# Rotary position products from one projection: exchanged halves are copied by ACT instead of made by PE

## The reference, cut to what matters

```python
var = jnp.mean(jnp.square(x), axis=-1, keepdims=True)
x_norm = x * jax.lax.rsqrt(var + EPS) * norm_scale
q = (x_norm @ Wq).reshape(b, seq, n_heads, dh)
k = (x_norm @ Wk).reshape(b, seq, n_heads, dh)
v = (x_norm @ Wv).reshape(b, seq, n_heads, dh)
q = apply_rope(q); k = apply_rope(k)
...
x1, x2 = jnp.split(x, 2, axis=-1)      # in apply_rope, per head
return jnp.concatenate([x1 * cos - x2 * sin, x1 * sin + x2 * cos], axis=-1)
```

## Time and profile before

| | |
|---|---|
| median of 3 runs | 2100.53 us (2097.97 to 2101.24) |
| profiled execution, its own time | 2096.08 us |
| its span, first to last instruction | 2094.2 us |
| mean granted TensorE clock | 0.903 of full |
| PE busy | 1725.3 us (82%) |
| DVE busy | 1591.4 us (76%) |
| ACT busy | 1014.0 us (48%) |
| POOL busy | 925.0 us (44%) |

### The profile page before, as it was taken

The page is one execution under the profiler, slowest core; times in us unless marked ns, Lnnn a source line. Parts: engine busy times, 40 slices in busy tenths (PEclk is TensorE's granted clock), DMA queues, the critical chain, the costliest instruction groups (busy, mean ns, idle before and its releaser), DMA issues.

```text
span 2094.2 us, 33718 instructions
## 1 busy us (share of the span) xinstructions
PE 1725.3 (82%) x12064; PEld 1120.0 (53%) x12141; DVE 1591.4 (76%) x3386; ACT 1014.0 (48%) x1997; POOL 925.0 (44%) x1166
## 2 busy tenths in 40 slices
PE   1465889989898989889798989989798989978785
PEld 0233446565565646465565646555565646555544
DVE  2666869889797979879696979879697978874522
ACT  1143363746455463646455473745445463735151
POOL 3335253636354463636344463636445453623112
PEclk9676789999898999989898999989899999989797
DMA  3001010000101010100101010000101010000100
GB/s 91 0 5 45 7 46 6 27 27 7 51 7 47 11 46 9 38 18 7 51 7 46 12 46 6 27 31 7 51 7 46 12 46 1 22 31 8 46 12 6
DMA packets 64617, 53.34 MB, mean 25 GB/s; under 512 B 6019, under 2 KB 63171, under 8 KB 64451
## 3 DMA queue, kind: packets, MB, share of 16 engines
q1 hardware_dynamic: 64450, 51.19, 7.9%
HBM read 8.44 MB, written 4.19 MB: 6 GB/s over the span
## 4 chain that ended last, share of the span: by engine, by line
PE 45%; DVE 25%; SPq 9%; issue 7%; ACT 5%; POOL 5%; DMA 4%; DVEq 0%; ACTq 0%; POOLq 0%
PE bank L872 42%; SPq L299 8%; DVE rmax L743 7%; DMA kh<-part 4%; PE bank L868 3%; DVE prob L823 2%; DVE tree L653 2%; DVE stats L644 2%; ACT prob L464 2%; DVE rmax L740 1%; DVE inner L653 1%; SPq L311 1%; POOL rstd L343 1%; ACT xch L480 1%; DVE kk L666 1%
## 5 line engine op out<-in xcount | busy, mean ns | idle before, releaser
L743 DVE TENSOR_REDUCE rmax<-bank 128x1 f32<-128x512 f32 (+2 forms) x768 | 355.7, 504 | 131.3 <-PE bank L872 130.9
L464 ACT ACTIVATE prob<-bank 128x512 f32<-128x512 f32 x640 | 354.4, 598 | 136.1 <-PE bank L872 131.0
L872 PE MATMUL bank<-kh,qh 72*128 72x512 bf16 (+3 forms) x1024 | 289.2, 332 | 93.2 <-DMA kh<-part 52.8
L430 POOL TENSOR_TENSOR prob<-xdT,spread 128x512 f32<-128x512 f32 x128 | 167.5, 1309 | 377.4 <-ACT spread L464 377.4
L872 PE MATMUL bank<-wexpT,prob 128*128 128x128 f32 x2048 | 272.1, 279 | 5.3 <-issue 4.1
L872 PE MATMUL bank<-qh,kh 75*128 75x512 bf16 (+3 forms) x1024 | 256.6, 305 | 22.7 <-ACT prob L464 19.6
L872 PEld LDWEIGHTS bank<-wexpT,prob 128*128 128x128 f32 x2048 | 255.2, 193 | 18.5 <-issue 12.4
L872 PEld LDWEIGHTS bank<-kh,qh 72*128 72x128 bf16 x1024 | 108.5, 106 | 211.4 <-DVE rmax L743 71.8
L464 ACT ACTIVATE spread<-bank 128x512 f32<-128x512 f32 x128 | 76.5, 597 | 296.0 <-PE bank L872 209.5
L690 DVE RECIPROCAL wkb<-wkb 128x512 f32<-128x512 f32 x64 | 213.3, 3332 | 0.5 <-POOL wkb L376 0.5
L872 PE MATMUL bank<-maskb,identb 128*128 128x128 bf16 x1024 | 210.8, 237 | 0.0
(11 more groups left out here) (212 smaller groups left out, 3556.9 us busy)
## 6 DMA issues: line engine op xcount, KB each, us to landing
qh<-part SPq DMA_DIRECT2D x144, 128.0 KB
kh<-part SPq DMA_DIRECT2D x144, 128.0 KB
x<-in_L_attn_x_dram SPq DMA_DIRECT2D x16, 256.0 KB, 2.9
out_dram<-yo SPq DMA_DIRECT2D x16, 256.0 KB, 3.0
qh<-maxT SPq DMA_DIRECT2D x16, 48.0 KB
wk<-in_L_attn_tm_Wk_dram SPq DMA_DIRECT2D x1, 256.0 KB
wv<-in_L_attn_tm_Wv_dram SPq DMA_DIRECT2D x1, 256.0 KB
wr<-in_L_attn_tm_Wr_dram SPq DMA_DIRECT2D x1, 256.0 KB
```

Source lines behind the costliest of these rows:

```text
L430: raised(pool.tensor_tensor(ug[:, e % 4, :], xdT[:, :], spread[e // 2 % 2][:, :], ALU.mult), "ug_side")
L464: raised(act.activation(dst, src, func, **kw), signal)
L743: last = dve.tensor_reduce(rmax[:, j, h:h + 1], S[n % 2][:, col:col + (j + 1) * P], AX_X, ALU.max)
L872: return pe.matmul(out_, w, x, start=start, stop=stop, **kw)
```

## The change

1. `w_rope` holds two weight tiles and not four. PE has two steps `rope0` (q, bank A0) and `rope1` (k, bank A1). ACT has two new steps, `rope_turn0` and `rope_turn1`, each of two activations of 64 rows by 512: rows 64 to 127 of the bank into rows 0 to 63 of an SBUF tile, and the reverse. They stand behind `exp25` and behind `exp26`. The sign is in the first half of `sin_t`, set once. DVE still makes four products: the cosine ones first (`rope_mul0`, `rope_mul1`, from the banks, each behind its `rope_turn`), then the sine ones (`rope_mul2`, `rope_mul3`, from the SBUF copies). DVE's order is not changed. `rope_sum0` waits for the third product, `rope_sum1` for the fourth.
2. `root_rms` becomes one affine step, one power and one product, and stands ahead of `root4`, not behind it.
3. `read_out` and `cmv` are four steps of four matmuls each, with a semaphore raise each. The four stand in direct succession in PE's order, and those who wait for them wait for all four.
4. Waits: `norm3` waits also for `xc` and `xch` of the sequence before, `gates0` for two `rope_mul` of it and not for four, `attn_v` for the first and not the third.
5. Nine steps `busy_...` for PE are defined; none of them is in PE's order.

The diff, cut to its core:

```diff
-        4:u5 ... 1:gated1 2:root4 2:root_rms 1:r_sig2 1:rwkv1 1:wk2
+        4:u5 ... 1:gated1 2:root_rms 2:root4 1:r_sig2 1:rwkv1 1:wk2
...
-        3:exp25 1:r_tanh3 3:exp26 3:exp27 3:exp28 3:exp29 2:part_hi0 2:part_hi1 3:exp30
+        3:exp25 2:rope_turn0 1:r_tanh3 3:exp26 2:rope_turn1 3:exp27 3:exp28 3:exp29 2:part_hi0 2:part_hi1 3:exp30
...
-        3:score24 3:score25 2:rope1 2:rope2 3:score26 3:score27 2:rope3 3:score28 3:score29
+        3:score24 3:score25 2:rope1 3:score26 3:score27 3:score28 3:score29
...
             def root_rms(b):
-                until(pool, b, "root4")
-                raised(pool.tensor_tensor(rms_a[:, :], mv[:, 4, :, 1], rstd[:, 4, :], ALU.mult), "rms_step")
+                until(pool, b, "moments4")
+                raised(pool.tensor_scalar(rms_a[:, :], mv[:, 4, :, 1], 1.0 + RMS_EPS, RMS_EPS * LN_EPS, ALU.mult, ALU.add), "rms_step")
+                raised(pool.tensor_tensor(minus[:, 4, :], mv[:, 4, :, 0], minus_one[:, :], ALU.mult), "rms_step")
                 until(pool, b, "rms_step", 1)
-                raised(pool.tensor_tensor(rms_b[:, :], rms_a[:, :], rstd[:, 4, :], ALU.mult), "rms_step")
-                until(pool, b, "rms_step", 2)
-                raised(pool.tensor_tensor(rms_a[:, :], rms_b[:, :], eps_rms[:, :], ALU.add), "rms_step")
+                raised(pool.tensor_tensor(rms_scale[:, :], rms_a[:, :], exponent[:, :], ALU.pow), "rms_step")
                 until(pool, b, "rms_step", 3)
-                raised(pool.tensor_tensor(rms_root[:, :], rms_a[:, :], exponent[:, :], ALU.pow), "rms_step")
-                until(pool, b, "rms_step", 4)
-                raised(pool.tensor_tensor(rms_scale[:, :], rms_root[:, :], rstd[:, 4, :], ALU.mult), "rms_step")
-                until(pool, b, "rms_step", 5)
                 raised(pool.tensor_tensor(rms_shift[:, :], minus[:, 4, :], rms_scale[:, :], ALU.mult), "rms_shift")
...
             def rope_sum(b, t):
-                until(pool, b, "rope_mul", 2 * t + 2)
+                until(pool, b, "rope_mul", t + 3)
...
+            def turn_dimensions(b, t):
+
+                until(act, b, "rope_ps", t + 1)
+                half = P // 2
+                act.activation(rope[2 * t + 1][0:half, :], (A0, A1)[t][half:P, :], ACT.Identity)
+                raised(act.activation(rope[2 * t + 1][half:P, :], (A0, A1)[t][0:half, :], ACT.Identity), "rope_turn")
...
             def rope_product(b, i):
-                until(dve, b, "rope_ps", i + 1)
-                raised(dve.tensor_tensor(rope[i], (cos_t if i % 2 == 0 else sin_t)[:, :], (A0, A1)[i % 2], ALU.mult), "rope_mul")
+                t = i % 2
+                if i < 2:
+                    until(dve, b, "rope_turn", t + 1)
+                    raised(dve.tensor_tensor(rope[2 * t], cos_t[:, :], (A0, A1)[t], ALU.mult), "rope_mul")
+                else:
+                    raised(dve.tensor_tensor(rope[2 * t + 1], sin_t[:, :], rope[2 * t + 1], ALU.mult), "rope_mul")
...
             def rope_product(b, i):
                 until(pe, b, "xcT")
                 until(pe, b, "yb")
-                if i >= 2:
-                    until(pe, b, "rope_mul", i - 1)
-                raised(mm((A0, A1)[i % 2], w_rope[:, i, :, :].rearrange("p d h -> p (d h)"), xcT[:, :]), "rope_ps")
+                raised(mm((A0, A1)[i], w_rope[:, i, :, :].rearrange("p d h -> p (d h)"), xcT[:, :]), "rope_ps")
```

More of the change, by code:

```diff
@@ L63 @@
         3:exp13 1:r_tanh2 3:exp14 3:exp15 3:exp16 3:exp17 3:exp18 3:exp19 2:norm_rms 3:exp20 3:exp21 2:xcT_out 1:k_exp3 3:exp22 3:exp23 1:k_first3 3:exp24
-        3:exp25 1:r_tanh3 3:exp26 3:exp27 3:exp28 3:exp29 2:part_hi0 2:part_hi1 3:exp30 3:exp31 2:part_mid0 3:exp32 3:pvT_out0 3:exp33 3:exp34 2:part_mid1
-        3:exp35 3:exp36 3:exp37 3:exp38 3:exp39 3:pvT_out1 2:norm4 3:attT_out 1:norm2 3:norm6 1:mix_before3 1:mix_before4 3:xdT_out 0:norm0 1:cmk_tanh0
-        3:route_exp 1:cmk_tanh1 1:cmk_tanh2 1:cmk_tanh3 2:values
+        3:exp25 2:rope_turn0 1:r_tanh3 3:exp26 2:rope_turn1 3:exp27 3:exp28 3:exp29 2:part_hi0 2:part_hi1 3:exp30 3:exp31 2:part_mid0 3:exp32 3:pvT_out0
+        3:exp33 3:exp34 2:part_mid1 3:exp35 3:exp36 3:exp37 3:exp38 3:exp39 3:pvT_out1 2:norm4 3:attT_out 1:norm2 3:norm6 1:mix_before3 1:mix_before4
+        3:xdT_out 0:norm0 1:cmk_tanh0 3:route_exp 1:cmk_tanh1 1:cmk_tanh2 1:cmk_tanh3 2:values
     """,
@@ L81 @@
         3:score16 3:score17 1:k3 3:score18 3:score19 3:weigh4 3:weigh5 3:score20 3:weigh6 3:score21 2:xcT 3:score22 1:r3 3:score23 3:weigh7 2:rope0
[L82 to L88, removed]
+        3:score24 3:score25 2:rope1 3:score26 3:score27 3:score28 3:score29 3:weigh8 3:weigh9 3:score30 3:weigh10 3:score31 3:weigh11 3:score32 2:attn_v
+        3:score33 3:score34 3:score35 3:score36 3:score37 3:back0 3:score38 3:score39 3:weigh12 3:weigh13 3:weigh14 3:weigh15 1:read_out0 1:read_out1
+        1:read_out2 1:read_out3 3:back1 3:attT 3:attn_out 1:xn2T 2:row0 3:xdT 2:row1 2:row2 3:centroids 1:cmk0 2:row3 2:row4 1:cmk1 1:cmk2 2:row5 2:row6
+        1:cmk3 2:row7 3:shared 1:cmr 2:row8 1:cmv0 1:cmv1 1:cmv2 1:cmv3 2:row9 3:gT 2:row10 3:gb0 2:row11 2:row12 3:gb1 0:xnT 3:biases 2:row13 3:gb2
+        2:row14 3:expert0 3:gb3 2:row15 2:row16 3:expert1 2:row17 3:gb4 2:row18 3:expert2 3:gb5 2:row19 1:xbT 3:gb6 2:row20 3:expert3 0:k0 2:row21 2:row22
+        1:gates0 0:v0 2:row23 1:gates1 2:row24 3:gb7 3:expert4 0:r0 2:row25 0:v1 3:gb8 2:row26 0:k1 3:expert5 3:gb9 2:row27 2:row28 3:expert6 2:row29
+        3:gb10 2:row30 3:expert7 2:row31 3:expert8 2:row32 2:row33 3:gb11 3:expert9 2:row34 2:row35 3:gb12 3:expert10 2:row36 2:row37 2:row38 3:gb13
+        2:row39 3:gb14 3:expert11 3:gb15 0:r1
     """,
@@ L551, in _ @@
                 "norm0": norm_first, "norm1": lambda b: (until(act, b - 1, "xn2T_ps"), norm(b, 1, hat, x1, "pre_hat")),
-                "norm2": lambda b: norm(b, 2, hat, x2, "post_hat"), "norm3": lambda b: norm(b, 3, xb, y0, "xb"),
+                "norm2": lambda b: norm(b, 2, hat, x2, "post_hat"), "norm3": lambda b: (until(act, b - 1, "xc"), until(act, b - 1, "xch"), norm(b, 3, xb, y0, "xb")),
                 "norm4": norm_tree, "norm_rms": norm_attention, "norm6": norm_experts, "norm7": norm_last,
@@ L927, in channel_gate, with channel_out @@
                 raised(last, "cmr_ps")
-            def channel_out(b):
-                until(pe, b, "silu")
-                by_tokens(T0, inner, cwv, "cmv_ps")
+            def channel_out(b, j):
+                if j == 0:
+                    until(pe, b, "silu")
+                raised(by_tokens(T0, inner, cwv, j), "cmv_ps")
             def turn_tree(b):
@@ L940, in gates @@
                 if k == 0:
-                    until(pe, b - 1, "rope_mul")
+                    until(pe, b - 1, "rope_mul", 2)
                 for j in range(2 * k, 2 * k + 2):
```

95 lines of the change are left out of this document (64 added, 31 removed).

## The result

The changed kernel takes 2133.2 us (median; 2128.05 to 2139.73), the kernel before beside it 2099.25 us: 1.0164 times as long, 95% interval 1.0138 to 1.019. Slower was right; 34 us against the 21 of the forecast was too little by more than a third, and the median lies just above the range.

The account below looks back on a forecast made before the run. No one engine was taken to bound the kernel; a turn is a ring of stretches, hanging on `score39`'s end. 15 x 1.5 us later, less 1.2, gave +21.3 on 2096.08; with the median's offset, 2121 us, range 2098 to 2133.

Parts of the forecast that it names:

- The question: When `score39` ends: whatever moves between `xcT` and `score39` moves the whole next turn by as much.
- The RMS root: On POOL, `rms_shift` 3.2 us earlier; `norm_rms` on ACT 1.16 us earlier, `xcT` on PE 0.80 us earlier.
- The replay: Step-by-step timing from `xcT` to `score39`: `exp30` 2.06 us late on ACT, `score39` 1.55 us later per turn.
- the price of the turned copies: Four 64x512 activations on ACT at 0.49 us each from start to start, 1.96 us in all.
- The upper bound of 0.60: Highest price for one turned copy on ACT, in us, if copies do not overlap; 0.24 was the lower bound.
- The standing of the sine product: `rope_mul3` on DVE stands until POOL's `rope_sum0` ends at 1109.20; 1.55 us later a turn with it, 0.8 without.
- The turn that was read: The full turn 1014.67 to 1134.02, 119.35 us, used as the base; `xch` to first DMA of q 19.29 us.
- The clock: Rival: PE's lower clock behind `row0` makes 5 of 15 turns 2 us longer, +10 us, 2131; chance 0.07.
- The edits at nothing: Split `read_out` and `cmv`, six more semaphore raises, changed waits: no cost; 1.6 us if one cost 0.1 a turn.
- The first turn: First of 16 sequences, bound by the chain over POOL to `read_out`: 1.2 us earlier (between 3.2 and 0).

Follow-up runs that it names:

- e_rms_only: The kernel before with only the new short `root_rms`, placed ahead of `root4`; ratio 0.9927 to the kernel before.
- e_sine_psum: The changed kernel with sine products read from the PSUM bank, not the SBUF copies, the exchange left out of the result; ratio 1.0133 to the kernel before.
- e_pieces: The kernel before with only `read_out` and `cmv` in four steps each and the added waits of `norm3`; ratio 1.0001 to the kernel before.
- e_one_copy: The changed kernel with one 128-row copy for each two of 64 rows, the exchange left out; 2113.65 us, ratio 1.0048 to the kernel before.
- e_late_parts_fill: The changed kernel with `part_hi0`, `part_hi1`, `part_mid1` later in ACT's order and eight matmuls in PE's gaps; 2136.25 us, ratio 1.015 to the kernel before.

## Why the prediction was right or wrong, point by point

- **The question.** That the end of `score39` decides and the rest of the turn follows held: the first DMA to `row0` changed by 0.25 us, `row0` to `yb` by 0.4, the stretch by 2.25.
- **The RMS root.** `xch` was forecast 1.16 us earlier and came 1.1 us earlier, without a wait. By itself the root is worth 1.0 us a turn, where the replay had 0.8: `exp24` starts 11.90 us behind `yb` with the short root, in `e_rms_only` and in the changed kernel alike, and 12.09 was forecast.
- **The replay.** Counted from `yb`, in the turn shown: `xch` 5.79 forecast and 5.78 measured, the first copy 13.06 and 13.01, the end of the second copy 16.09 and 16.54, the end of the second sine product 19.44 and 19.77, `part_hi1` 20.89 and 21.21, `exp30` 21.39 and 21.75, the first DMA 27.8 and 28.3. The mechanism and its order were right to the last step; sizes were off. The median lies 0.2 us beyond the range, which is far less than the runs of one kernel differ, but it is 12 us beyond the forecast.
- **The step that failed: the price of the turned copies**, put at 0.49 us from start to start ("the rows are free"). The two of a pair lie 0.61 apart, and so do the first of them and the step ahead of it, and the second and the step behind it. From `exp24` to the end of the second copy the replay had 4.00 us and the kernel takes 4.64; `exp24` gave 0.19 of it back, and 0.45 are left. The 48-row copy in the trace of before has the right duration, but it stands alone, and so says nothing on overlap. The upper bound of 0.60 was written down and never carried through the replay. Put there for the four copies, it makes the last copy start 0.33 us later, so 1.9 a turn and not 1.55, about 5 us more in the sum. The upper end of the range, 2133, was that sum with the clock on top, and would have moved by the same 5 us. This is the largest single term of the miss, and not half of it.
- **The standing of the sine product** was right: 1.40 us for 1.48, on the same meeting with `rope_sum0`, and 0.7 us a turn at full clock by `e_sine_psum`. The product starts 0.43 us behind the sum, for 0.44 in the replay; that was not luck, since the late copies moved both by the same 0.4 us. What the Trainium skill says in page "SBUF — State Buffer", section "SBUF: two separate sides", of a DVE instruction with two SBUF inputs against a GpSimd one that reads SBUF, these traces agree with: inside POOL's sum the product takes 1.40 us with two SBUF inputs and 0.68 with one.
- **The turn that was read.** I took the turn of 19.29 from `xch` to the first DMA as the typical one; 13 of the 15 have 19.15. That is 0.15 us a turn, 2 us.
- **The clock** was a rival, in the wrong place: behind `row0`, where it was no different in kind, and not behind the two new gaps of PE. It costs 0.2 us a turn in the changed kernel, 3 us. That PE "now has less work" was the right premise. In the replay ACT's steps from `exp25` to `exp27` follow each other without a gap, so that PE has to wait for them in the middle of the stretch, and I did not ask what these waits do to the clock.
- **The edits at nothing.** The pieces and the waits of `norm3` cost nothing by `e_pieces`.
- **The first turn** was forecast 1.2 us earlier; its `row0` is 0.6 us earlier (197.37 and 196.74).

The sum by these terms, a turn: 1.55 of the replay; plus 0.36 at `exp30`, which is the 0.45 of the copies less 0.08 for the shorter standing; 0.15 for the turn that was read; 0.2 for the clock. That is 2.26, for 2.25 measured. That the copies hold up `exp30` through `part_hi1` is shown by edits (`e_one_copy`, `e_sine_psum`, `e_late_parts_fill`); the split of the miss into these terms is read from the traces.

## What to carry to other kernels

When work moves from an engine that seems busy to one that seems to have gaps, the gaps may be the first engine's time: replay the orders step by step, carry both ends of every unknown price through the replay, and not only through the sum. Here a step in ACT's order that waits (`part_hi1`) held up a step that did not need it; but taking that away showed PE's lower clock right behind it, so look for the second in line before promising the gain. Order has a price of its own too: three steps other than exponentials, put in a row on ACT, cost 1.0 to 1.3 us a turn. Undo a mixed change part by part: here 1 us a turn was gained by one part and 3.2 lost by another, and the good part with one move of the order gives a kernel 1.2% faster than the one it came from.

## What the runs showed of the hardware that was not expected

- ACT steps of 128 rows that read a bank and follow each other without a wait start 0.47 to 0.50 us apart in these traces, though each lasts about 0.60. Two copies of 64 rows from and to different halves start 0.60 to 0.61 apart, and a full step starts 0.61 to 0.62 behind such a copy. A copy of 64 rows lasts 0.59 us, as long as one of 128. It starts 0.48 behind a full step ahead of it when it keeps its rows, and 0.61 to 0.62 when it crosses to the other half.
- In the changed kernel PE has two gaps of 1.8 and 1.3 us, with 0.5 us of scores between them, in a stretch that had been at the higher clock throughout, and then the lower one for 3.4 us (0.51 granted), in 13 turns of 15. With eight matmuls of 128x512 bf16 in the gaps there was none in that stretch in 15 turns. Such a piece cost 0.2 us a turn in the changed kernel, where it lies beside ACT's wait for POOL, and 1.3 in `e_one_copy`, where it lies behind it.
